# The last two feed-forwards of a gated cross-attention stack: from batch after batch within each matmul layer to batches in turn

## The reference

```python
# stage 3: x = x + tanh(g_xattn[1]) * _L1_xattn(LN(x), ctx)
#   inside, for the second attention block (a2), on x1 = LN(first block):
x_out = x1 + o @ li1_w + li1_b                          # attention output, o from cross attention
h     = gelu(LN(x_out, ln3_g, ln3_b) @ li2_w + li2_b)   # 128 -> 512
a2    = x_out + h @ li3_w + li3_b                       # 512 -> 128
# the block returns x1 + a2, so
x = x + tanh(g_xattn[1]) * (x1 + a2)
# stage 4: x = x + tanh(g_ffn[1]) * _L1_ffn(LN(x))
y     = LN(x)
probs = softmax(y @ Wr.T)                               # 8 experts, the last one is used
h     = gelu(y @ W1[7] + b1[7])                         # 128 -> 512
x     = x + tanh(g_ffn[1]) * (h @ W2[7] + b2[7]) * probs[:, 7]
```

## Time and profile before

| | |
|---|---|
| median of 3 runs | 401.43 us (396.87 to 401.79) |
| profiled execution, its own time | 401.46 us |
| span of its instructions | 399.7 us |
| mean granted clock of TensorE | 0.934 of full |
| last attention's last matmuls start | 353.89 us |
| first matmuls of `a2f`, batch 0, start | 355.11 us |
| last result operation of DVE ends | 397.28 us |

### The profile page before, as it was taken

How to read it: one execution, slowest core, us unless ns; L and a number is a source line. 1 busy time by engine, 2 the same in 40 slices (tenths; PEclk the granted TensorE clock), 3 DMA queues, 4 the chain that set the end, 5 groups by cost and what they waited for, 6 DMA issues and landing times.

```text
span 399.7 us, 6860 instructions
## 1 busy us (share of the span) xinstructions
PE 333.6 (83%) x2134; PEld 235.4 (59%) x2134; DVE 287.3 (72%) x740; ACT 269.2 (67%) x953; POOL 121.6 (30%) x227
## 2 busy tenths in 40 slices
PE   4889998546396969998998899898948999878796
PEld 4868886313145545565655565675634888746456
DVE  0678679677559986898989989646566887854505
ACT  3478897477156797989989899424237789834160
POOL 1326664248103332332323333210122434420200
PEclk9999999967597898999999999999986999999799
DMA  6900000000049598106943973000000000000001
GB/s 193 343 10 1 2 2 0 1 2 2 0 109 210 116 202 180 27 2 125 212 86 65 211 159 150 2 2 2 0 1 2 1 2 1 2 0 2 0 0 52
DMA packets 6907, 24.74 MB, mean 62 GB/s; under 512 B 1451, under 2 KB 1528, under 8 KB 6136
## 3 DMA queue, kind: packets, MB, share of 16 engines
q1 hardware_dynamic: 6872, 24.31, 25.4%
HBM read 7.00 MB, written 0.52 MB: 19 GB/s over the span
## 4 chain that ended last, share of the span: by engine, by line
PE 45%; DVE 22%; ACT 18%; issue 5%; DMA 5%; POOL 2%; SPq 1%; DVEq 0%; ACTq 0%
ACT pring L1222 8%; PE ps L444 8%; PE ps L523 7%; PE ps L543 7%; PE ps L596 5%; PE ps L579 5%; DVE nm L1599 4%; PE ps L725 3%; DVE xn L1298 3%; ACT arena L1096 3%; ACT arena L1205 2%; DVE stats L1283 2%; PE ps L675 2%; PE ps L689 2%; DVE arena L1389 2%
## 5 line engine op out<-in xcount | busy, mean ns | idle before, releaser
L1222 ACT ACTIVATE pring<-ps,nm 128x512 f32<-128x512 f32 x128 | 88.7, 721 | 4.8 <-DVE nm L1599 4.8
L1599 DVE TENSOR_REDUCE nm<-ps 128x1 f32<-128x512 f32 x128 | 81.3, 679 | 14.5 <-PE ps L689 14.5
L1096 ACT ACTIVATE arena<-ps,nmx 128x77 f32<-128x77 f32 x256 | 79.1, 343 | 16.7 <-DVE nmx L1373 16.5
L982 POOL TENSOR_SCALAR_AFFINE_SELECT pring<-pring 128x128 f32<-128x128 f32 x128 | 37.1, 293 | 89.8 <-ACT pring L1222 89.8
L689 PE MATMUL ps<-stack 128*128 128x512 f32 x128 | 54.3, 489 | 7.4 <-ACT pring L1222 5.5
L1096 ACT ACTIVATION_READ_ACCUMULATOR arena<-ps,nmx 128x1 f32 x256 | 57.2, 223 | 0.0
L950 POOL TENSOR_TENSOR arena<-arena,rden 128x616 f32<-128x616 f32 x32 | 39.2, 1224 | 53.8 <-DVE rden L1382 53.8
L444 PE MATMUL ps<-ident,pring 128*128 128x128 f32 x320 | 47.9, 280 | 6.9 <-ACT arena L1205 5.6
L444 PEld LDWEIGHTS ps<-ident,pring 128*128 128x128 f32 x320 | 37.6, 143 | 20.8 <-POOL pring L982 9.8
L543 PEld LDWEIGHTS ps<-arena 128*128 128x128 f32 x320 | 39.2, 192 | 14.1 <-DVE arena L1389 12.4
L543 PE MATMUL ps<-arena 128*128 128x128 f32 x320 | 42.4, 280 | 5.7 <-DVE arena L1389 5.7
(11 more groups left out here) (144 smaller groups left out, 522.5 us busy)
## 6 DMA issues: line engine op xcount, KB each, us to landing
stack<-sides SPq DMA_DIRECT2D x32, 256.0 KB, 5.0
stack<-arena SPq DMA_DIRECT2D x16, 256.0 KB, 5.0
stack<-hid SPq DMA_DIRECT2D x12, 256.0 KB, 5.3
wa_sb<-in_wa SPq DMA_DIRECT2D x1, 1536.0 KB, 14.7
early<-in_w SPq DMA_DIRECT2D x2, 512.0 KB, 7.9
stack<-hid SPq DMA_DIRECT2D x8, 128.0 KB, 2.5
arena<-in_wa SPq DMA_DIRECT2D x1, 1024.0 KB, 4.8
pring<-in_wf SPq DMA_DIRECT2D x1, 768.0 KB, 10.3
```

What stands on the lines that cost most here:

```text
L982: pool.affine_select(out=blk, in_=blk, compare_op=ALU.is_gt, fill=0.0, base=0, pattern=[[1, P]], channel_multiplier=-1).then_inc(masked, 1)
L1096: ins = act.activation(Pc[:, i % PC_SLOTS, h * HS:h * HS + M], bank(where[key])[:, h % 4 * HS:h % 4 * HS + M], ACT.Exp, bias=nmx[:, i % 4, ...
L1222: release(act.activation(pring[:, n % 2, i, :], bank(f"S{i}"), ACT.Exp, bias=nm1[:, n % 8, i:i + 1], accum_out=den1[:, n % 8, i:i + 1]), ( ...
L1599: dve.tensor_reduce(nm1[:, n % 8, i:i + 1], bank(f"S{i}"), AX.X, ALU.max, negate=True).then_inc(nm1_ready, 1)
```

## The change

- `ffn` is split in `ffn_up` (the first matmuls) and `logits`, so that they can be placed apart.
- PE's order in the last two feed-forwards becomes: first matmuls of `a2f` 0, transposes of `a2f` 1, second matmuls of `a2f` 0, first of `a2f` 1, half of the second of `a2f` 1, transposes of `f1` 0, the other half, first of `f1` 0, logits 0, half of the second of `f1` 0, transposes of `f1` 1, the other half, first of `f1` 1, logits 1, second of `f1` 1.
- ACT does all four gelu of a batch, then copies the other batch's transposes; for the first block's feed-forward (`a1f`) the old place inside the gelu stays.
- DVE does the three residual steps of `a2f` for each batch by itself (`a2_residual`): those of batch 0 ahead of its output, those of batch 1 between the statistics and the normalising of `f1` 0. Then come output 1, statistics 1 and normalise 1 of `f1`.

The number of matmuls, transposes, copies and gelu is as it was. The three residual operations were already one instruction for each batch; their waits come for each batch now. The diff, without the part in which `ffn` is cut in two and a call in the first block is renamed:

```diff
             ln_transposes("a2", 0)
             cross("a2")
-            ffn("a2f", 0)
+            ffn_up("a2f", 0)
             ln_transposes("a2f", 1)
-            ffn("a2f", 1)
             ffn_down("a2f", 0)
-            ffn_down("a2f", 1)
-
-
+            ffn_up("a2f", 1)
+            ffn_down("a2f", 1, range(0, 2))
+            ln_transposes("f1", 0)
+            ffn_down("a2f", 1, range(2, NT))
             pe.wait_ge(loaded["wf1"], 16)
-            ln_transposes("f1", 0)
-            ffn("f1", 0)
+            ffn_up("f1", 0)
+            logits(0)
+            ffn_down("f1", 0, range(0, 2))
             ln_transposes("f1", 1)
-            ffn("f1", 1)
-            ffn_down("f1", 0)
+            ffn_down("f1", 0, range(2, NT))
+            ffn_up("f1", 1)
+            logits(1)
             ffn_down("f1", 1)
...
-            def gelu(site, b, names=None):
+            def gelu(site, b):
                 for k in range(NF):
-                    if k == 2 and b == 0:
+                    if site == "a1f" and k == 2 and b == 0:
...
-            for site, names in (("a2f", ("a2_ln3_g", "a2_ln3_b")), ("f1", None)):
-                if site == "a2f":
-                    preload(ACT.Gelu)
-                else:
-                    ln_evac(site, 0, names)
-                gelu(site, 0, names)
-                gelu(site, 1)
+            preload(ACT.Gelu)
+            gelu("a2f", 0)
+            ln_evac("a2f", 1, ("a2_ln3_g", "a2_ln3_b"))
+            gelu("a2f", 1)
+            for b in range(NB):
+                ln_evac("f1", b)
+                gelu("f1", b)
             preload(ACT.Exp)
...
+            def a2_residual(b, step):
+                if step == 0:
+                    did(dve.tensor_tensor(xb[:, b, :, :], x1[:, b, :, :], row4("a2_li3_b"), ALU.add))
+                elif step == 1:
+                    did(dve.tensor_tensor(xb[:, b, :, :], xb[:, b, :, :], xo[:, b, :, :], ALU.add))
+                else:
+                    did(dve.scalar_tensor_tensor(r[:, b, :, :], xb[:, b, :, :], tg[:, 1:2], r[:, b, :, :],
+                                                 ALU.mult, ALU.add))
+                settle()
...
             ln_stats("a2f", 1, xo)
             ln_norm("a2f", 1, xo)
-            bias_and_residual("a2_li3_b")
-            for b in range(NB):
-                did(dve.scalar_tensor_tensor(r[:, b, :, :], xb[:, b, :, :], tg[:, 1:2], r[:, b, :, :],
-                                             ALU.mult, ALU.add))
-            settle()
...
-            ln_both("f1", a2_out, r)
+            for step in range(3):
+                a2_residual(0, step)
+            a2_out(0)
+            ln_stats("f1", 0, r)
+            for step in range(3):
+                a2_residual(1, step)
+            ln_norm("f1", 0, r)
+            a2_out(1)
+            ln_stats("f1", 1, r)
+            ln_norm("f1", 1, r)
```

More of the change, by code:

```diff
@@ L570, in cross, with ffn_up @@
                         filled(pe.matmul(bank("B")[:, 0:3], ones[:, :], wsum[:, :], start=True, stop=True), "wsum")
-            def ffn(site, b):
+            def ffn_up(site, b, parts=range(NF)):
                 w1, w2, _ = FFN_W[site]
                 pe.wait_ge(xnT_ready, nthT(site, b))
-                for k in range(NF):
+                for k in parts:
                     res = f"S{k}"
@@ L580, in ffn, with logits @@
                            ("up", site, b, k))
[L581 to L586, removed]
+            def logits(b):
+                claim(pe, "T0", ("logits", b), read_by=(logits_ready, b + 1))
+                for t in range(NT):
+                    m = pe.matmul(bank("T0")[:, t * 8:(t + 1) * 8], xnT[:, b, t * P:(t + 1) * P],
+                                  wf1_sb[:, 2 * HID:2 * HID + 8], start=True, stop=True)
+                filled(m, ("logits", b))
             def ffn_down(site, b, tiles=range(NT)):
@@ L812, in down_beside_fold @@
                 return pair_issued
-            ffn("a1f", 0)
+            ffn_up("a1f", 0)
             ln_transposes("a1f", 1)
             fold("a2", 0, down_beside_fold(0))
-            ffn("a1f", 1)
+            ffn_up("a1f", 1)
             fold("a2", 1, down_beside_fold(1))
@@ L1113, in cross @@
                         ln_evac("a2f", 0, ("a2_ln3_g", "a2_ln3_b"))
-            def gelu(site, b, names=None):
+            def gelu(site, b):
                 for k in range(NF):
-                    if k == 2 and b == 0:
-                        ln_evac(site, 1, names)
+                    if site == "a1f" and k == 2 and b == 0:
+                        ln_evac("a1f", 1, ("a1_ln3_g", "a1_ln3_b"))
                     key = ("up", site, b, k)
@@ L1238, in _ @@
             preload(ACT.Gelu)
-            gelu("a1f", 0, ("a1_ln3_g", "a1_ln3_b"))
+            gelu("a1f", 0)
             gelu("a1f", 1)
@@ L1645, in _ @@
             cross("a2")
-            add_to_xb(1, "a2")
-            ln_stats("a2f", 1, xo)
-            ln_norm("a2f", 1, xo)
-            bias_and_residual("a2_li3_b")
-            for b in range(NB):
-                did(dve.scalar_tensor_tensor(r[:, b, :, :], xb[:, b, :, :], tg[:, 1:2], r[:, b, :, :],
-                                             ALU.mult, ALU.add))
-            settle()
             def a2_out(b):
@@ L1660, in a2_out @@
                 settle()
-            ln_both("f1", a2_out, r)
+            add_to_xb(1, "a2")
+            ln_stats("a2f", 1, xo)
+            ln_norm("a2f", 1, xo)
+            for step in range(3):
[8 more added lines that the diff above has]
+            ln_norm("f1", 1, r)
             for b in range(NB):
```

## The result

| | before | after |
|---|---|---|
| median | 398.0 us (20 runs, 396.54 to 402.32) | 396.32 us (20 runs, 395.08 to 397.85) |
| profiled execution, its own time | 401.46 | 397.19 |
| span | 399.7 | 394.4 |
| first matmuls of `a2f` 0 start | 355.11 | 354.01 |
| last gelu ends | 388.80 | 384.23 |

The ratio of after to before is 0.9934, with a 95% interval of 0.9905 to 0.9963: faster, by less than the 2% that would count as a difference. The forecast was 397.3 us, 393.8 to 400.8, and no change beyond 2%.

The account below looks back on a forecast made before the run. PE was the chain, with holes waiting for DVE and ACT; removing the 2.14 us hole, 2.9 of half clock and copy waits, about half given back, nets 4.13 less: 401.46 becomes 397.3 us, range 393.8 to 400.8.

Parts of the forecast that it names:

- the sum: Prediction's step-by-step addition along PE from 359.98, then DVE's end: 393.15 instead of 397.28, so 4.13 us less.
- The new wait: PE, after the first matmuls of `a2f` 1, waits for the fourth gelu: 4.42 - 3.44 = 0.98 us.
- the pieces that were put to nothing: Hidden ACT copies, POOL's power for `f1` 0 beside DVE, PE's `wf1` wait, batch 0's residual steps: no cost expected.
- Given back: About half the gain lost: 3.58 us of `f1` 0's second matmuls now ahead of the last gelu, plus a 0.98 wait.
- These two steps cost 2.9 us: Transposes and first matmuls of `f1` 0 at half clock before: 1.09 instead of 0.63 and 6.17 instead of 3.70 us.
- a general shift: Whole runs moving like the one at 396.87, 4.6 us below; chance 0.07.
- The held port: Rival: POOL's power and batch 1's residual steps hold each other, delaying `f1` 0's transposes 0.84 us; 398.2 us, chance 0.15.
- these transposes have no slack: Transposes of `f1` 0: normalising ends at 370.1, PE asks at 370.21, so each delay goes straight to the end.
- its two rows: POOL beside DVE's normalising: a power left it at 1.11 us; a large scaling made it 1.64 instead of 1.11.
- The rivals in which it falls in spite of the new order: PE's clock halves: one stretch, 3.3 us, 400.6 us, chance 0.13; swinging, two stretches, 6.6 us, 403.9 us, chance 0.05.
- left it at 1.00: Argument for full clock: 1.27 us of PE idle before 359.98 had not lowered the granted clock.
- A stretch of half clock was priced at half its length: A PE stretch like 374.5 to 381.2 was taken to cost about half its 6.7 us, 3.3.

Follow-up runs that it names:

- f1_firsts: Changed kernel with PE's old order in `f1`: second matmuls of batch 0 again behind the first matmuls of batch 1; median 395.47 us, ratio to before 0.9913.
- exp_early: Changed kernel with batch 0's exponentials, gate, gated bias and result taken while PE works on `f1` 1; median 392.80 us (5 runs), ratio to before 0.9864.
- before_exp_early: Kernel before, with batch 0's exponentials, gate, gated bias and result taken while PE works on `f1` 1; median 398.52 us, ratio to before 0.9985.
- hole_filled: Kernel before plus nine unread matmuls in PE's idle time ahead of the transposes of `f1` 0; median 397.77 us, ratio to before 0.9987.
- before_again: Kernel before, unchanged, run and profiled once more; median 397.67 us, profiled execution 396.58 us.
- f1_only: Changed kernel with `a2f` back in the order of before, so only `f1` alternates; median 400.68 us, ratio to before 1.0057.

## Why the prediction was right, and where its size was off

- **The path step by step.** From the transposes of `a2f` 1 to the last gelu it forecast 385.30 - 359.98 = 25.32; it is 384.23 - 358.89 = 25.34. From there to DVE's last result it forecast 7.85; it is 7.71. Every step in between lies within 0.12 us of the sum, so the agreement isn't errors that cancel. The new wait was forecast at 0.98; it is 0.78, mostly because the sum let PE be through 3.44 us after it started on the first matmuls, and the record has 3.60. All of the pieces that were put to nothing (copies, the power, `wf1`, the residual steps of batch 0) cost nothing.
- **Given back.** 3.58 us of second matmuls ahead of the last gelu, and the end passing from PE to softmax and gate: shown by `f1_firsts` (without the former the last gelu 2.08 earlier, the end 1.32), `exp_early` (without the latter 2.59 faster) and `before_exp_early` (no gain where PE ends last).
- **The baseline: the term that was mis-sized.** "This execution lies 0.03 from the median of the runs shown, 401.43, so nothing has to be converted." The median of three runs lies in the upper group, as the profiled execution does, and only 24 of 90 runs are of that group. The 2.9 us of "These two steps cost 2.9 us" is right for that execution (2.93, `hole_filled` and `before_again`), but three quarters of the runs don't seem to have it to lose. So the forecast of 4.13 less came true for the pair of profiles and is more than double the 1.7 of the medians. Against the usual execution the change gains 1.31. The one run at 396.87, which the prediction noted and set aside as a general shift, was the usual case.
- **The absolute time.** 397.3 was forecast, 396.32 measured. The stage is 0.11 shorter than forecast; the rest lies ahead of 355 us and around the span, where the kernels don't differ. That the median came as near as 0.98 is in part luck: the sum took over the first 355.11 us of one execution, and the other profiles reach the same place at 352.57 to 354.94. The 2% that the prediction called about what a measurement can tell was far too wide: the interval of the ratio is 0.3% to either side.
- **The held port.** It was given a chance of 0.15 and 0.84 us. The power was held 0.37, the residual steps not at all (0.68 and 0.69, as when alone), so nothing came to the end. "So these transposes have no slack" was wrong: PE asked for them at 369.19, and `xn` was there at 368.80, 0.39 us earlier where the sum had 0.1. The residual steps took 2.19 (365.45 to 367.64) instead of 2.3, and they began 0.17 ahead of the power and not with it. The prediction also set its two rows apart by the form of DVE's instruction; both are the normalising, and what differs between them is POOL's instruction (128x616 against 128x4). The Trainium skill, "SBUF — State Buffer", section "Who interferes with whom", has whichever comes later stand still until the other is done. Here POOL's power was longer beside DVE, as that would have it, but DVE's next addition, which started at 366.16 while the power ran until 367.00, wasn't longer. So this pair shows the hold in one direction only.
- **The clock.** The rivals in which it falls in spite of the new order didn't come: the granted clock is 1.00 from 354 to 388. But their argument, that 1.27 us of idle "left it at 1.00", held for the profile that I had; `before_exp_early` fell behind those very waits. The changed kernel keeps the 1.27, and whether it ever falls there is open; none of its 20 runs is above 397.85. A stretch of half clock was priced at half its length; that of before is 6.8 us by the earlier trace rows (374.4 to 381.2) and cost 2.93, so less than half.

## What to carry to other kernels

Where an execution has a stretch at half clock, ask first whether the median execution has it too: take the baseline from several runs, and forecast the order's gain and the clock's gain apart. When two batches alternate, work that lay behind the last step of the critical chain moves ahead of it, so look what ends last afterwards and take the next piece out of that chain in the same edit: here batch 0's softmax, worth twice what the whole change gains at full clock. A transpose whose copy takes 0.6 us, as here, belongs inside a run of matmuls, not at its end.

## What the runs showed of the hardware that was not expected

The same idle time of PE, 2.14 and 2.15 us at the same place of the same kernel, was followed by 6.8 us of half clock in one execution and by none in another; and waits of 1.27 and 0.87 us left the clock at full in four profiles (both of before, `hole_filled`, `f1_only`) and were followed by half clock in one (`before_exp_early`). POOL's power of 4 columns, 1.01 us alone, took 1.38 beside a DVE addition of two SBUF tensors (0.68 us), while DVE's next addition, which ran beside the power, took 0.69, as the same step of batch 0 did with POOL idle.
